# The next pass's first projections inside this pass: reordering the attention tail of a one-core transformer layer

## The reference

```
ada = cond @ ada_w + ada_b                       # shift, scale, gate for both halves
x1  = ln(x) * (1 + scale1) + shift1
q, k, v = split(x1 @ qkv_w + qkv_b)              # 16 heads of 128
x2  = x + gate1 * (softmax(q k' / sqrt(128)) v @ out_w + out_b)
x3  = x2 + gate2 * ffn(ln(x2) * (1 + scale2) + shift2)      # 256 -> 1024 -> 256, gelu
x4  = x + minGRU(x3)                             # a recurrence over 32 tokens
y   = 32 Runge-Kutta steps driven by x4          # 4 stages each, tanh(q) @ coupling
out = x4 + block-sparse ffn(y)                   # 4 of 16 blocks kept per token
```

## Time and profile before

| what | value |
|---|---|
| median of 3 runs | 516.93 us (515.63 to 517.02) |
| the profiled execution | 515.61 us, of which the span from first to last instruction is 513.8 us |
| mean granted TensorE clock | 0.970 |
| busy: PE, DVE, ACT, POOL | 449.6 us (88%), 434.9 us (85%), 316.3 us (62%), 48.6 us (9%) |
| chain that ended last | DVE 42%, PE 40%, ACT 6%, issue 5%, POOL 4% |

### The profile page before, as it was taken

The page is one execution under the profiler, slowest core; times in us unless marked ns, Lnnn a source line. Parts: engine busy times, 40 slices in busy tenths (PEclk is TensorE's granted clock), DMA queues, the critical chain, the costliest instruction groups (busy, mean ns, idle before and its releaser), DMA issues.

```text
span 513.8 us, 13730 instructions
## 1 busy us (share of the span) xinstructions
PE 449.6 (88%) x4980; PEld 307.5 (60%) x4980; DVE 434.9 (85%) x1705; ACT 316.3 (62%) x880; POOL 48.6 (9%) x77
## 2 busy tenths in 40 slices
PE   2999989998999899997498997689888888888887
PEld 2655665567556665575244443667676766766666
DVE  4969786787777876889988786999999999999994
ACT  1387855786487748786458755465655646555563
POOL 3010330224021211123000000000000000000000
PEclk9999999999999999999789999698989999999999
DMA  8972402200202000000000000000000000000000
GB/s 294 417 311 63 106 7 76 61 21 0 82 21 62 0 0 1 0 1 0 0 1 1 0 1 0 3 3 0 1 1 11 11 1 10 1 11 11 1 10 22
DMA packets 10127, 20.82 MB, mean 41 GB/s; under 512 B 1456, under 2 KB 4720, under 8 KB 9456
## 3 DMA queue, kind: packets, MB, share of 16 engines
q1 hardware_dynamic: 9536, 19.89, 11.2%
q10 hardware_dynamic: 560, 0.60, 0.3%
HBM read 19.40 MB, written 1.08 MB: 40 GB/s over the span
## 4 chain that ended last, share of the span: by engine, by line
DVE 42%; PE 40%; ACT 6%; issue 5%; POOL 4%; DMA 1%; ACTq 0%; DVEq 0%
PE bank L804 34%; DVE base L1649 5%; DVE lin L1751 5%; POOL ptx L477 4%; DVE qs L1655 4%; DVE cub L1643 3%; PE score L804 3%; DVE sq L1637 3%; DVE pacc L1761 3%; PE spare L804 2%; ACT ao_sb L541 2%; DVE thlo L1633 1%; DMA vec<-vecs 1%; DVE qn L1655 1%; DVE acc L1421 1%
## 5 line engine op out<-in xcount | busy, mean ns | idle before, releaser
L804 PE MATMUL bank<-x,pairs_store 128*128 128x512 f16 x384 | 85.6, 379 | 0.0
L804 PE MATMUL score<-th,coup_part 128*128 128x32 f16 x1024 | 47.2, 179 | 18.1 <-ACT th L788 17.2
L804 PEld LDWEIGHTS bank<-x,pairs_store 128*128 128x128 f16 x384 | 37.1, 98 | 42.8 <-DVE x L1219 0.4
L477 POOL TENSOR_TENSOR ptx<-pt,ptx 32x256 f16<-32x256 f32 x64 | 44.7, 699 | 189.4 <-ACT ptx L573 185.8
L541 ACT ACTIVATE big<-bank,pass_b 128x512 f16<-128x512 f32 x64 | 42.1, 684 | 24.3 <-DVE pass_b L1347 14.4
L788 ACT ACTIVATE th<-qs 128x64 f16<-128x64 f32 x96 | 24.5, 255 | 47.5 <-DVE qs L1655 47.5
L804 PEld LDWEIGHTS score<-th,coup_part 128*128 128x128 f16 x1024 | 34.7, 97 | 31.1 <-ACT th L788 29.7
L1359 DVE SCALAR_TENSOR_TENSOR big<-bank,pass_b,big 128x512 f16<-128x512 f32 x64 | 45.7, 742 | 8.0 <-ACT big L541 7.3
L804 PE MATMUL bank<-pairs_store,ao_sb 128*128 128x256 f16 x384 | 46.6, 273 | 4.7 <-DVE acc L1421 1.4
L804 PEld LDWEIGHTS bank<-pairs_store,ao_sb 128*128 128x128 f16 x384 | 35.5, 97 | 13.6 <-issue 3.6
L804 PE MATMUL bank<-pairs_store,x 128*128 128x512 f16 x192 | 43.4, 379 | 0.0
(11 more groups left out here) (210 smaller groups left out, 1041.8 us busy)
## 6 DMA issues: line engine op xcount, KB each, us to landing
wqk_sb<-wqk SPq DMA_DIRECT2D x16, 256.0 KB, 3.0
wv_sb<-wv SPq DMA_DIRECT2D x4, 512.0 KB, 5.6
wo_sb<-wo SPq DMA_DIRECT2D x4, 512.0 KB, 4.2
f_sb<-ffn_w SPq DMA_DIRECT2D x2, 1024.0 KB, 14.2
ao_sb<-xtok SPq DMA_DIRECT2D x4, 256.0 KB, 6.1
big<-ada_w SPq DMA_DIRECT2D x1, 1024.0 KB, 9.7
x_sb<-xT SPq DMA_DIRECT2D x1, 1024.0 KB, 13.3
w_sb<-w1T SPq DMA_DIRECT2D x1, 1024.0 KB, 16.4
```

The source lines that it names most:

```text
L477: nc.gpsimd.tensor_tensor(ptx[s, 1, :, s], pt[s], ptx[s, 0, :, s], ALU.subtract).then_inc(ptx_ready, 1)
L804: return nc.tensor.matmul(dst, lhsT, rhs, start=start, stop=stop, **kw)
```

## The change

The queries and keys of a pass's first head are projected in the pass before: two banks behind `out_project(0, 1)`, two behind the second part of `out_project(1, 1)`; those of the very first head ahead of all passes. The evictions follow on ScalarE and VectorE, and so do the first four weight splits of the next pass, one inside the fourth projection and three ahead of head 3's values. The numbering of bank uses is shifted accordingly. In passes 1 to 3 all four strips of head 3's scores are copied by ScalarE. In all passes the fourth head's rows are placed between head 2's two value banks, and GpSimd's low rows wait for the second of these. TensorE's last pass is written out behind a loop of three, and has number lists of its own. Biases are scaled once for all 16 heads (`head_b`). Behind the passes, 6, 15 and 20 matmuls are added whose results nobody reads.

```diff
 NBANK = 5
-USE_PROJ = [0, 10, 16, 22]
-USE_V = [4, 5, 6, 7, 8, 9, 14, 15]
-USE_PV = [20, 26, 30, 35]
-USE_OUT = [[28, 29, 32, 37], [33, 34, 38, 39]]
+USE_V = [0, 1, 2, 3, 4, 5, 10, 11]
+USE_PROJ = [[26, 27, 38, 39], [6, 7, 8, 9], [12, 13, 14, 15], [18, 19, 20, 21]]
+USE_PV = [16, 22, 28, 33]
+USE_OUT = [[24, 25, 30, 35], [31, 32, 36, 37]]
+LAST_PV = [16, 22, 26, 31]
+LAST_OUT = [[24, 25, 28, 33], [29, 30, 34, 35]]
+FIRST_USES = (0, 1, 1, 1, 1)
...
 # GpSimd
                 def place_low(j):
+                    if j == QUAD - 1:
+                        use = (LAST_PV if i == NQUAD - 1 else USE_PV)[j - 1] + 1
+                        pool.wait_ge(full[bank_of(use)], i * NPAR + count_of(use))
...
 # ScalarE, end of a pass
-                copy_scores(3, NB4 // 2)
+                copy_scores(3, NB4 // 2 if last else NB4)
                 place_high(2)
                 exps(3)
-                empty_pv(2)
+                if not last:
+                    empty_next_proj(0, 1)
+                empty_pv(2, [0])
                 place_high(3)
-                if i == NQUAD - 1:
+                empty_pv(2, [1])
+                if last:
                     mlp_highs(5, 7)
+                else:
+                    for t in range(1, 4):
+                        weights_high(i + 1, t)
                 empty_pv(3)
-                if i == NQUAD - 1:
+                if last:
                     mlp_highs(7, 8)
+                else:
+                    empty_next_proj(2, 3)
...
 # TensorE
+                def project_next(*ks):
+                    if last:
+                        return
+                    if ks[0] == 0:
+                        pe.wait_ge(split_ready, i * NSPLIT + NSPLIT + 1)
+                    for k in ks:
+                        projection(USE_PROJ[0][k], 0, k, fill(USE_PROJ[0][k]))
...
-                project(0)
                 values(0, 1)
...
                 out_project(0, 1, [0, 1])
+                project_next(0, 1)
                 mix(2)
...
                 out_project(1, 1, [3])
+                project_next(2, 3)
                 out_project(1, 2, [2, 3])
                 out_project(1, 3, [2, 3])
+
+            with pe.Fori(0, NQUAD - 1) as i:
+                attention_pass(i, False)
+            attention_pass(NQUAD - 1, True)
...
+            def unread(dst, count):
+                for _ in range(count):
+                    mm(dst, scaled_eye[:], ptx[:, 0, 0:G // 2].rearrange("p g n -> p (g n)"), True, True)
...
             turn_x2(0)
+            unread(spare[:], 6)
             turn_normed(0)
+            unread(spare[:], 15)
...
             last_gates()
+            unread(score[:, 1], 20)
...
 # VectorE, end of passes 1 to 3
+                    low_pv(1, [1])
+                    shift(3)
+                    add_heads(0, 0)
+                    add_heads(0, 1)
+                    normalise(3)
+                    low_first_head(0, (i + 1) * QUAD)
+                    low_first_head(1, (i + 1) * QUAD)
+                    low_pv(2)
+                    add_heads(0, 2)
+                    low_weights(i + 1, 1, 2, 3)
+                    low_pv(3)
+                    add_heads(0, 3)
+                    add_heads(1, 0)
+                    add_heads(1, 1)
+                    low_first_head(2, (i + 1) * QUAD)
+                    low_first_head(3, (i + 1) * QUAD)
+                    add_heads(1, 2)
+                    add_heads(1, 3)
```

More of the change, by code:

```diff
@@ L532, in _ @@
             act.wait_ge(ptx_cleared, 1)
+            act.wait_ge(bias_ready, 3)
+            for k, use in enumerate(USE_PROJ[0]):
+                h, w = k // 2, k % 2
+                act.wait_ge(full[bank_of(use)], 1)
+                nc.scalar.activation(qk_sb[:, 0, w, 0, h * HALF:(h + 1) * HALF], bank[bank_of(use)][:], ACT.Identity,
+                                     bias=head_b[:, w, 0:1]).then_inc(high_ready, 1)
             for i in range(NQUAD):
@@ L581, in empty_values @@
                         high(USE_V[g], v_sb[:, g, 0])
[L583 to L595, removed]
+                empty_values(0)
+                if last:
+                    mlp_highs(0, 1)
                 empty_values(1)
+                if last:
+                    mlp_highs(1, 2)
                 copy_scores(0)
@@ L603, in _ @@
                 empty_values(5)
+                if last:
+                    mlp_highs(3, 4)
                 empty_projs(1, (0, 1))
@@ L840, in _, with projection, attention_pass @@
             ada_chunks(spare[:, D:], 3 * KB, 6 * KB).then_inc(ada2_summed, 1)
-            with pe.Fori(0, NQUAD) as i:
+            def projection(use, j, k, dst):
+                h, w = k // 2, k % 2
+                weights = wqk_pair[:, j % 2].rearrange("p c (k w d) -> p c k w d", k=KB, w=2)
+                sum3(dst[:], [(weights[:, :, n, w], x1_pair[:, :, n, h * HALF:(h + 1) * HALF]) for n in range(KB)]
+                     ).then_inc(full[bank_of(use)], 1)
+            pe.wait_ge(split_ready, 1)
+            for k, use in enumerate(USE_PROJ[0]):
+                pe.wait_ge(x1_ready, k // 2 + 1)
+                pe.wait_ge(free[bank_of(use)], 1)
+                projection(use, 0, k, bank[bank_of(use)])
+            def attention_pass(i, last):
                 def fill(use):
@@ L853, in project @@
                     pe.wait_ge(split_ready, i * NSPLIT + SPLIT_ORDER.index(("qk", j)) + 1)
[L854 to L861, removed]
+                    for k, use in enumerate(USE_PROJ[j]):
+                        projection(use, j, k, fill(use))
+                def project_next(*ks):
+                    if last:
+                        return
+                    if ks[0] == 0:
+                        pe.wait_ge(split_ready, i * NSPLIT + NSPLIT + 1)
+                    for k in ks:
+                        projection(USE_PROJ[0][k], 0, k, fill(USE_PROJ[0][k]))
                 def scores(j):
@@ L865, in scores @@
                         pe.wait_ge(scores_copied, i * (QUAD * NB4) + NB4 * j)
+                    else:
+                        for use in USE_V[1:5]:
+                            fill(use)
                     for g in range(G):
-                        if g % 4 == 0:
-                            taken(USE_PROJ[j] + g // 2)
-                            taken(USE_PROJ[j] + g // 2 + 1)
+                        if j and g % 4 == 0:
+                            taken(USE_PROJ[j][g // 2])
+                            taken(USE_PROJ[j][g // 2 + 1])
                         q, k = (qk_sb[:, j % 2, w, :, g * P:(g + 1) * P] for w in range(2))
@@ L901, in mix @@
                                       False, g % 4 == 3, skip_group_check=True)
-                        last.then_inc(full[bank_of(USE_PV[j] + h)], 1)
+                        last.then_inc(full[bank_of(use_pv[j] + h)], 1)
                 def out_project(pair, c, js):
-                    use = USE_OUT[pair][c]
+                    use = use_out[pair][c]
                     first, end = js[0] == 2 * pair, js[-1] == 2 * pair + 1
@@ L1256, in close_heads @@
             def close_heads(c):
[L1258 removed]
+                use = LAST_OUT[0][c]
                 if c == 0:
@@ L1413, in low_pv @@
                         hi, lo = (ao_pair[:, j, c, h * HALF:(h + 1) * HALF] for c in range(2))
-                        low(USE_PV[j] + h, hi, lo, pass_b[:, 2, j:j + 1])
+                        low((LAST_PV if last else USE_PV)[j] + h, hi, lo, head_b[:, 2, i * QUAD + j:i * QUAD + j + 1])
                 def add_heads(pair, c):
-                    use = USE_OUT[pair][c]
+                    use = (LAST_OUT if last else USE_OUT)[pair][c]
                     a = pair_of(c)
@@ L1485, in _ @@
                     last_heads(2)
-                assert own.n == STEPS and pairs[0] == PAIRS
+                assert own.n == STEPS and pairs[0] == (i + 1) * PAIRS + (0 if last else 4)
             own.n, own.base = start + NQUAD * STEPS, 0
```

114 lines of the change are left out of this document (69 added, 45 removed).

## The result

The changed kernel takes 510.34 us, the median of four runs (509.59 to 510.66), against 516.97 us for the kernel before in the same session (515.63 to 517.22): ratio 0.9875, 95% interval [0.9854, 0.9896]. Forecast were 509.8 us, between 506.8 and 513.4. The profiled execution took 510.63 us, with a span of 508.8 us (513.8 before), so there is 5.0 us to account for between the two traces.

A forecast was written before the change was run, and what follows sets the result against it. TensorE was taken to bound each pass, with slack only in its tail. Gains of 5.9 (tails) + 0.3 (last pass) + 0.2 (scan) = 6.4 us gave 509.2 or 510.5, taken as 509.8 us, range 506.8 to 513.4.

The forecast's parts named there:

- TensorE is the bound in a pass and its tail has slack: Attention pass: 52.2 us of TensorE work in 55.96 us, with 3.8 us of holes, all behind the last scores.
- The tail, step by step: Second pass's tail followed in clock times: next values start at 136.63 instead of 138.61, 1.98 us a tail, 5.9 for three.
- The new holes: In the tail: 0.57 us inside mix(3), waiting for VectorE, and 0.84 us before out_project(1, 0, [3]).
- two of the rivals: Tail: both new holes double, about 514.0 us (chance 0.15); or stalls do not occur, about 505.6 us (0.07).
- its own check by holes: Tail: 3.7 us of holes become 0.22 + 0.2 + 0.57 + 0.84 = 1.83.
- Last pass: Fourth pass's tail: fourth head's rows placed 0.6 us earlier, eating VectorE's idle time; gain 0.3 us, between 0 and 0.66.
- Unread matmuls: Before the hidden layer and the scan: they hold the clock at 2.4 GHz, worth 0 and 0.2 us.
- The 0.2 us for the scan: Scan's first 7.06 us at low clock: VectorE bounds it; gain between 0 and 3.5 us, taken as 0.2.
- the step behind them: Ahead of the scan, 318.3 to 325.19: 20 unread matmuls, 4.3 us, should hold the clock at 2.4 GHz for the next work.
- the reason that carried the term: Scan's start: VectorE is full (6.92 of 7.06 us) and so bounds it, also in the warm stretch behind.
- The loop: TensorE's last pass written out behind a loop of three: no price for a turn, so none for one fewer.
- The slower rival: Written-out fourth pass starves TensorE once each 55 matmuls, eight stops of 1 us: 517.6 to 518 us (chance 0.04).

The follow-up runs named there:

- e2: The changed kernel with VectorE emptying head 3's two value banks ahead of the next pass's three weight splits instead of behind them: 508.07 us, ratio 0.9852.
- e3: The changed kernel with ScalarE emptying both of head 2's value banks before placing the fourth head's rows, in all passes: 510.62 us, ratio 0.9897.
- e5: The changed kernel with the second half of the next pass's first projections behind the last two output chunks, VectorE's order likewise: 512.45 us, ratio 0.9925.
- e9: e8 with one of the second half's two projections moved ahead of mix(3), banks and ScalarE's and VectorE's orders matched: 506.59 us, ratio 0.9819.
- e1: The changed kernel without its 41 unread matmuls (6, 15 and 20): 510.12 us, ratio 0.9883.
- e6: The changed kernel with 31 unread matmuls ahead of the scan instead of 20: 510.30 us, ratio 0.9883.
- e4: The changed kernel with TensorE's first three passes written out too, instead of a loop of three: 510.13 us, ratio 0.9887.
- e8: e2 with a pass's first scores waiting for two freed banks ahead of each half, not all four ahead of the first: 507.44 us, ratio 0.9827.
- e10: The changed kernel once more, unaltered, against the kernel before: 510.14 us, two runs (510.6 and 509.68), ratio 0.9881.

## Why the prediction was right, and where it was off

*TensorE is the bound in a pass and its tail has slack.* Right. The pass less its 52.2 us of work leaves 3.8 us of holes before and 1.9 now; the view of waits, which counts less of each hole, lists 2.2 us for TensorE before and 1.1 now, from values to values of the second pass. The pass became shorter by what the holes lost.

*The tail, step by step.* Each place was met to 0.13 us. The changed kernel's tail runs 0.90 us earlier in its trace than the old one's (scores 114.34, 115.24). Forecast and measured starts, the latter with 0.90 added: output projection 116.80 and 116.79, projections 119.39 and 119.41, `mix(2)` 121.98 and 122.00, `mix(3)` 126.1 and 126.17, its second part 127.12 and 127.17, `out_project(1, 0, [3])` 130.15 and 130.23, values 136.63 and 136.76. The new holes were put at 0.57 and 0.84 us; they are 0.55 (125.27 + 0.45 = 125.72 to 126.27) and 0.86. So the holes were neither twice as large nor absent, as two of the rivals had them. The step that was off is the one that chose 1.98 us a tail over its own check by holes, 3.7 - 1.83 = 1.87: along the chain small differences add up to the 0.13 us at the end. Measured are 1.83 to 1.85, so 5.5 us and not 5.9.

*The cause of each hole.* e2 takes away the second one by VectorE's order alone (508.07 us). e3 shows that the placing of the rows, costed at a hole of 0.57 us, costs the tail nothing: without it GpSimd's rows are the wait, and the sum of the two holes is the same. e5 shows for the second half of the projections that they earn by what they stand over, and e9 by adding cover where a hole was. That the first half covers the two holes of `mix(2)` (0.62 and 0.82 us before, none after) is read from the two traces; no run moves that half alone.

*Last pass.* 0.3 us forecast between 0 and 0.66, measured 0.44. The mechanism was the named one (e3: 0.52 us lost without it).

*Unread matmuls.* Nothing in the hidden layer: forecast and shown (e1). The 0.2 us for the scan were not there, and the step behind them, that 20 unread matmuls ahead of the idle stretch hold the clock into the scan, failed: it fell to 0.57 within 320.19 to 327.25. e6 keeps it up and still gains nothing, so the reason that carried the term, VectorE is full, was the right one.

The Trainium skill (TensorE: Matmul & The Clock Gate, HAM oscillation) counts throttled time as lost by the ratio of the clocks. e1 (510.12 us) and e6 (510.30), against 510.34, do not agree with it here, where another engine ends both stretches.

*The loop.* Nothing was forecast and nothing measured: 54.12 us a pass in the loop, 54.12 and 54.11 written out (e4). The slower rival falls with it; no run shows a stop of the kind that it supposed, once each 55 matmuls.

*Missed.* The start. The prediction had no term for it, and the trace shows 0.93 us lost: the first scores come 20.95 us behind the landing of the vectors (8.79) and not 19.65, 1.30 us more, less 0.37 for an earlier landing. In this execution the low clock accounts for the 1.30: the first projection's 24 matmuls last 6.86 us (20.29 to 27.15) against 5.30 before (20.92 to 26.22), 1.56 more, and they begin 0.26 us sooner behind the landing. The scores then follow the values without a wait (27.15 + 2.59 = 29.74). The change has a cost of its own at this place, which the slow projection hides here. Its scores wait for all four first banks ahead of their first half: 0.56 us in e2, e4 and e6, 0.38 in e3, all with a fast clock, and none in e8, which waits by halves. So with a fast clock the scores come at 20.22 us (19.85 in e3), with a low one at 20.71 to 20.95 (the changed kernel, e1, e5 and e10).

Sum: 6.4 forecast, - 0.4 (tails) + 0.14 (last pass) - 0.2 (scan) - 0.93 (start) = 5.0, which is the difference of the spans. The forecast of 509.8 us is closer to the measured median, 510.34, than these terms are: it started from 516.2, between the old kernel's median and its traced execution, and took 6.4 us off, where the traces account for 5.0 and the medians for 6.6. As far as it rests on the 1.6 us between the last two, which no trace explains, the close hit is luck.

## What to carry to other kernels

Work with no wait of its own is worth at most the hole that it stands over, less what it delays: 0.61 us a pass for two old holes of 1.04 together (e5), 0.38 for a piece moved over a hole of 0.55, since a new one of 0.39 came behind it (e9). Place it in pieces, one over each hole (e9: 506.59 us, against 507.44 for e8 with the same work in two halves). In an engine that runs in order, look at what stands ahead of the eviction that the matmuls wait for: three splits that nobody wanted yet cost 0.66 us a pass here (e2). When a wait goes, look who is second: rows placed earlier gave GpSimd's wait away and took VectorE's, and a third wait behind both kept the tail's length (e3). Where a clock is low, follow the first result to its reader before pricing it: if the reader waits for another engine, as at 260.3 us here, the low clock costs nothing.

## What the runs showed of the hardware

The granted clock under the first projection of one and the same instruction stream was 0.50 in the changed kernel and 1.00 in e6 (22 to 24 us), with TensorE busy on small f32 products in both until the projection (in e6 with a gap of 0.22 us just ahead of it; e3 had 1.00 without such a gap):

```profile
22.00:24.00 2.00, 2.00 (x6) 0.72 (x5) 2.00 (x4) 1.00 (x2) 0.00 (x0) 0.50 0.98 414
```
```profile
22.00:24.00 2.00, 1.01 (x6) 0.28 (x5) 1.91 (x4) 1.48 (x3) 0.00 (x0) 1.00 1.04 438
```

And the clock can fall after the work has begun: with TensorE idle from 317.6 to 320.19 it was 1.00 in the scan's first microsecond and 0.56 in the next; with unread matmuls until 319.75 it stayed at 1.00 until 326 and was 0.50 in the three microseconds behind.
